# Attention with a residual and two layer norms on one Trainium2 core: the order of scores and value products, of three VectorE steps, and the engine that cuts a lower part

## The reference

```
q = x @ wq.T + bq;  k = x @ wk.T + bk;  v = x @ wv.T + bv
scores = q·k / sqrt(32), causal;  weights = softmax(scores)
x1 = layernorm(x + (weights @ v) @ wo.T + bo)
out = layernorm(x1 + quantised_scale_and_clip(x1) @ quantised_scale_and_clip(w_ffn) * rescale)
```

## Time and profile before

| | |
|---|---|
| median of 3 runs | 2452.48 us (2452.33 to 2453.8) |
| the profiled execution | 2451.5 us, of it 2449.8 us from the first to the last instruction (the span) |
| busy over the span | PE 96%, PEld 61%, DVE 76%, ACT 54%, POOL 37% |
| batches 0 to 19, without fillers | first exp at 445.41 us, first exp of batch 20 at 556.26 us |
| batches 20 to 271 | 556.26 us to about 2031 us |

### The profile page before, as it was taken

One profiled execution on the slowest core, in us unless ns is written; L12 is line 12 of the kernel. 1 busy time (PEld: TensorE's weight loads), 2 busy tenths in 40 slices (PEclk: granted clock), 3 DMA queues, 4 the chain that ended last, 5 costly groups with the idle time before them and its releaser, 6 DMA issues.

```text
span 2449.8 us, 35663 instructions
## 1 busy us (share of the span) xinstructions
PE 2347.4 (96%) x13933; PEld 1488.8 (61%) x13933; DVE 1859.7 (76%) x1387; ACT 1319.6 (54%) x1443; POOL 918.0 (37%) x472
## 2 busy tenths in 40 slices
PE   6999998789999999999999999999999998999998
PEld 5778776335555555555555555555555556888887
DVE  6655665788888888888889998888888886444444
ACT  2232224577777777777777676777777773100000
POOL 2553453013233233234232323332324323666563
PEclk9999999899999999999999999999999999999999
DMA  7775767231222112212221122212221212222221
GB/s 234 260 254 204 278 241 258 60 62 36 53 57 66 44 45 66 66 45 58 53 66 44 44 55 63 58 44 61 53 63 44 66 61 112 91 89 86 86 94 61
DMA packets 159958, 231.55 MB, mean 95 GB/s; under 512 B 9582, under 2 KB 109902, under 8 KB 157774
## 3 DMA queue, kind: packets, MB, share of 16 engines
q1 hardware_dynamic: 136206, 178.27, 25.1%
q10 hardware_dynamic: 23616, 51.39, 5.5%
HBM read 140.50 MB, written 89.13 MB: 94 GB/s over the span
## 4 chain that ended last, share of the span: by engine, by line
PE 64%; DVE 7%; ACT 5%; POOL 3%; issue 2%; DMA 0%; ACTq 0%; DVEq 0%; POOLq 0%
PE bank L1365 18%; PE bank L1377 16%; PE bank L1440 14%; PE bank L1350 12%; ACT prob L838 4%; DVE acc L1117 4%; POOL att_lo L689 2%; PE bank L1387 2%; PE bank L1430 1%; DVE acc L1113 1%; PE bank L1395 1%; POOL prob L684 1%; DVE r_den L1077 1%; ACT att_hi L825 1%; DVE r_hi L1079 0%
## 5 line engine op out<-in xcount | busy, mean ns | idle before, releaser
L838 ACT ACTIVATE prob<-bank 128x1024 f32<-128x1024 f32 x1088 | 1055.4, 1023 | 422.5 <-PE bank L1365 394.7
L1117 DVE TENSOR_TENSOR acc<-acc,prob 128x2048 f32<-128x2048 f32 x420 | 987.4, 2351 | 71.4 <-ACT prob L838 48.6
L1365 PE MATMUL bank<-q_st,keys 98*128 98x512 f32 x2176 | 646.8, 416 | 16.5 <-ACT prob L838 13.3
L1365 PEld LDWEIGHTS bank<-q_st,keys 98*128 98x128 f32 x2176 | 376.5, 189 | 352.9 <-ACT prob L838 258.4
L1377 PE MATMUL bank<-prob,v_t 128*32 128x512 f32 x4352 | 526.2, 601 | 0.0
L684 POOL TENSOR_SCALAR_AFFINE_SELECT prob<-prob 128x1024 f32<-128x1024 f32 x128 | 204.1, 1617 | 591.6 <-ACT prob L838 591.6
L1377 PEld LDWEIGHTS bank<-prob,v_t 128*32 128x32 f32 x4352 | 114.0, 109 | 263.4 <-issue 251.9
L1113 DVE TENSOR_TENSOR acc<-prob 128x2048 f32<-128x2048 f32 x60 | 141.5, 2358 | 118.5 <-ACT prob L838 78.7
L1259 PE MATMUL bank<-xt_hi,w_hi 128*128 128x512 f32 x512 | 204.8, 400 | 19.1 <-DVE xt_lo L921 15.3
L1350 PE MATMUL bank<-wo_hi,att_hi 128*128 128x512 f32 x512 | 209.1, 408 | 11.9 <-POOL att_lo L689 8.5
L869 ACT ACTIVATE xs_hi<-bank 128x1024 fp32r<-128x1024 f32 x32 | 32.9, 1027 | 336.3 <-DVE y L900 261.5
(11 more groups left out here) (132 smaller groups left out, 2643.2 us busy)
## 6 DMA issues: line engine op xcount, KB each, us to landing
q_st<-q_hi_d SPq DMA_DIRECT2D x128, 256.0 KB
xt_raw<-x_t SPq DMA_DIRECT2D x16, 1024.0 KB, 6.6
q_hi_d<-part_hi ACTq DMA_DIRECT2D x64, 256.0 KB, 2.7
q_lo_d<-part_lo ACTq DMA_DIRECT2D x64, 256.0 KB, 3.2
x_row<-x SPq DMA_DIRECT2D x32, 512.0 KB, 4.6
xb_d<-x_row SPq DMA_DIRECT2D x32, 512.0 KB, 2.7
q_st<-q_lo_d SPq DMA_DIRECT2D x64, 256.0 KB
res<-xb_d SPq DMA_DIRECT2D x32, 512.0 KB, 5.7
```

What stands on the lines that cost most here:

```text
L838: nc.scalar.activation(prob[:, s % SLOTS, 2 * p:2 * p + 2], bank[:, 2 * p:2 * p + 2], ACT.Exp, scale=SCALE).then_inc(p_done, 1)
L1117: nc.vector.tensor_tensor(acc[:, n % 2], acc[:, n % 2], new, ALU.add).then_inc(acc_done, 1)
L1365: last = nc.tensor.matmul(bank[:, g].rearrange("p (a n) -> p a n", n=P), keys[:, k // QT, k % QT * P:(k % QT + 1) * P], queries[:, :, g], ...
```

## The change

Three edits, all in attention. (1) Batches 1 to 19 and 271, which have no fillers, put the value product of step 2u-2 between the two scores of the batch. (2) VectorE's `add_residual` of both halves stands right behind the addition into `acc`, ahead of `invert` and `normalise_group`; the moments stay behind them. (3) `att_lo` is made by VectorE in the same steps (behind `normalise_group`, ahead of the moments) and no longer by GpSimd. No instruction is added or dropped.

```diff
@@ gpsimd, step loop
-                if s in split_at:
-                    q = split_at[s]
-                    pool.wait_ge(att_hi_cut, q + 1)
-                    nc.gpsimd.tensor_tensor(att_lo[q % 2][:], att[:, q % TILES_KEPT], att_hi[q % 2][:].bitcast(F32), ALU.subtract).then_inc(att_cut, 1)
@@ vector
+            def lower_attended(q):
+
+                dve.wait_ge(att_hi_cut, q + 1)
+                nc.vector.tensor_tensor(att_lo[q % 2][:], att[:, q % TILES_KEPT], att_hi[q % 2][:].bitcast(F32), ALU.subtract).then_inc(att_cut, 1)
+
             for s in range(STEPS):
...
+                if s in sum0_at:
+                    add_residual(sum0_at[s], 0)
+                if s in sum1_at:
+                    add_residual(sum1_at[s], 1)
                 if s % 2 == 0 and s // 2 in group_of_den:
                     invert(group_of_den[s // 2])
                 if s % 2 == 0 and s // 2 - 1 in group_of_den:
                     normalise_group(group_of_den[s // 2 - 1])
-                if s in sum0_at:
-                    add_residual(sum0_at[s], 0)
+                if s in split_at:
+                    lower_attended(split_at[s])
                 if s in sum1_at:
                     q = sum1_at[s]
-                    add_residual(q, 1)
                     dve.wait_ge(y_read, 2 * q + 2)
                     moments_of(res[:, q % 2], stats[:, q % 2], moments[:, q % 2], ln1, q * LN)
@@ tensor
             for u in range(BATCHES):
                 scores(2 * u)
                 between(u)
+                single = u >= 1 and u not in fillers
+                if single:
+                    weigh_values(2 * u - 2)
                 scores(2 * u + 1)
+                if u >= 1 and not single:
+                    weigh_values(2 * u - 2)
                 if u >= 1:
-                    weigh_values(2 * u - 2)
                     weigh_values(2 * u - 1)
```

More of the change, by code:

```diff
@@ L1141, in _ @@
             lower_wf(0)
-            dve.wait_ge(att_hi_cut, LAST_B + 1)
-            nc.vector.tensor_tensor(att_lo[LAST_B % 2][:], att[:, LAST_B % TILES_KEPT], att_hi[LAST_B % 2][:].bitcast(F32), ALU.subtract).then_inc(att_cut, 1)
+            lower_attended(LAST_B)
             for i in range(1, 4):
```

## The result

The changed kernel takes 2436.68 us (2435.89 to 2438.43, four runs), the kernel before 2452.4 us in four (2449.0 to 2453.8): ratio 0.9936 [0.9919, 0.9953], so it is faster by 0.6%, clear of noise. The forecast was -7.2 us; this is -15.7. The profiled execution took 2435.89 us, span 2434.1, against 2449.8 before.

What follows compares the result with a forecast made beforehand. No engine was full in batches without fillers; with fillers TensorE was the limit, 98% busy. Terms -8.5 + 3 + 3 - 7 + 2 + 0.3 = -7.2 us took 2451.5 to 2444.3, median 2445.3 us; range 2434 to 2452.

Steps and rivals of the forecast that it cites:

- Edit 1: Batches 1 to 19: value products between scores make VectorE the limit, 4.79 us a batch instead of 5.36; -8.5 us.
- The term of 0.8 for the start: Start of attention at the slow clock: a product between scores lets VectorE's addition of step 4 start 0.8 us earlier.
- Edit 3 (a): Step 4 of a pair: the lower part stands in VectorE's queue, so TensorE's filler starts 0.2 us later each; +3 us.
- Edit 3 (b): Behind step 4, VectorE's delay may last until step 12's half-0 sum, which frees the projection's bank; 0.3 in ten pairs, +3.
- Edit 3 (c): Part with fillers: GpSimd no longer stretches VectorE's additions or queues masks behind `att_lo`; -5 and -2, together -7 us.
- lower bound of -15.3: Most that the end of GpSimd's hold on VectorE could gain: TensorE's waits on `att_lo` and on the inverses.
- Edit 2: Sums first free the bank earlier but make the inverse 0.65 later where both share a step, three times late; +2 us.
- Tail: Last additions: one stretched by 0.9 under `att_lo` gives way to a lower part of 1.22; +0.3 us.
- A: Rival: nearly all stretch and mask waits in the filler part reach TensorE; -8.5 and another -10, 2434 us; chance 0.16.
- B: Rival: masks and inverses interlock with the new order, so single steps gain only 2.5 us; 2450 us; chance 0.12.
- C: Rival: VectorE's queue at step 4 delays the filler by a full 1.22, half again at step 12; +14, 2466; chance 0.06.
- D: Rival: exchange between GpSimd and VectorE doesn't help, VectorE's net load of 13.1 us falls on the path; 2457; chance 0.06.

Runs made afterwards that it cites:

- product_ahead: Changed kernel with the value product of a batch without fillers put ahead of the denominators and the spreading; 2431.33 us, ratio 0.9921.
- changed_old_sums: Changed kernel with the sums put back behind invert and normalise; 2435.82 us, ratio 0.9932 to the kernel before.
- lower_only: Kernel before with only `att_lo` moved to VectorE, behind `normalise_group`; 2437.97 us, ratio 0.9937.
- hold_read: Changed kernel in which GpSimd also does its old subtraction into a spare tile that nothing reads; 2506.13 us, ratio 1.0223.
- hold_write: Changed kernel in which GpSimd also fills a spare tile by memset, writing only; 2435.66 us, ratio 0.9936.
- best_old_sums: Changed kernel with value product ahead of denominators, first tile's split at step 3, sums back in their old place; 2430.73 us, ratio 0.9914 (2426.22 with sums first).
- lower_and_sums: Changed kernel with the old order of batches, value products not between the scores; 2439.91 us, ratio 0.9939.

## Why the prediction was right in direction and half in size

**Edit 1** (predicted -8.5; measured -7.1, and -6.8 to the first filler). Size near; a step was wrong: "VectorE doesn't ... It becomes the limit", 4.79 a batch. TensorE and ScalarE went at their own rate, 4.50 against the 4.45 I worked out, since exp waits only for the addition of four steps earlier. VectorE's lag was a debt, paid at each group's end: 1.80, 1.78 and a fall of the clock. product_ahead won 2.6 of it by covering the wait. The term of 0.8 for the start was small: the slow clock itself ended 3 to 4 us earlier, and batch 1 alone is 1.9 shorter. Batch 20's first exp stood at 551.57; less the 2.4 of the untouched stretch 549.1, just outside the 546 to 549 announced.

**Edit 3 (a)** (+3; measured +0.4 at place 3). The count was right, the filler at 0.1 behind the lower part; VectorE's four operations overlap at their ends by a little, so it was 0.08 in the pair shown instead of 0.2.

**Edit 3 (b)** (+3; measured nearly 0). Four batches grew by 0.4, and in changed_old_sums three of those got it back, so in these it was not this debt but edit 2; the fourth, 162, is the only 0.4 that lower_only shows. The wait that the debt was to lengthen, a half projection for the sum of the half before, is 3.1 us in four places in both kernels.

**Edit 3 (c)** (-7; the failed step). With (b) at zero it is -11.6 in the changed kernel, -11.9 alone. The step was "in the rest, where the split falls on an addition, 2.0 of stretch goes and 1.22 comes, worth -2 together". I netted the stretch against the new operation as two durations on VectorE. But 2.0 against 1.22 is not what counts: four additions later the stretched kernel was late for the end of a group, there met GpSimd's mask too, and the denominators or the inverse were late for TensorE; the 1.22 us ended in time. Those eleven batches gave 11.0 us and not 2. The other part of the term, four pairs with the mask right behind the split at 1.2 each, -5, was too large: there are three, and they gave 1.8 together. Nor did VectorE's waits for masks go away with `att_lo`: 39.8 us in 21 places before, 33.7 in 18 in the changed kernel, 40.3 in 21 in lower_only. My lower bound of -15.3 was made of two of TensorE's waits and left out the third row of the same view, 7.8 us of denominators waiting for the last addition, which went entirely; the inverses fell by 4.5. The wait on `att_lo`, the largest that I named, gave nothing (8.5 before; 11.3 under "issue" after).

The Trainium skill's rule ("SBUF — State Buffer", "Who interferes with whom") is borne out in both halves: hold_read's GpSimd read stretched additions to 4305 ns; beside hold_write's memset the longest is 2992, as in the changed kernel without it. The "might not help" of the Trainium skill's "Perfetto Trace Analysis", "Optimizing Scalar/DVE Operations", is not: the exchange from GpSimd to VectorE, lower_only, gave -12.0 us in batches 20 to 270.

**Edit 2** (+2; measured +0.5 inside the change, +2.5 alone by twelve runs, where falls of the clock enlarge it). The inverse was late where the prediction said, in three batches of 0.4. It missed that the earlier sum is probably worth 0.6 at place 3 once the lower part is early too (best_old_sums).

**Tail** (+0.3; measured -0.2). Within what that stretch varies.

**The rivals.** A came nearest, in size (-7.1 and -10.8 for its -8.5 and -10) and in its sign, over 6 us gained from batch 20 on. Of its mechanism the half on the stretched additions is what happened; the half on the mask waits is not, as they hardly changed. B fell (7.1 us gained before batch 20), C fell (place 3 cost 0.03 a pair, not 0.9), D fell with lower_only.

What stays open: what decides whether a wait of TensorE is followed by a fall of the clock. The spreading's 1.80 at 498.34 was not, 1.78 at 534.61 was. Nor does it take a wait of that length: the fall at 471 us in the kernel before comes among plain batches, whose longest wait is the 0.73 of the earlier trace rows.

## What to carry to other kernels

Ask of a stretched operation not how much longer it is but which semaphore the bound engine waits for next behind it: a short operation that comes out even can end in time where a stretch of like size ends late. Move an operation with two inputs off GpSimd when VectorE is about to run adds and casts whose end is waited for, or at least away from a group's end, and look again for what then comes to wait. On an engine that works in order, put independent work ahead of the instruction that waits.

## What the runs showed of the hardware

- A short wait of TensorE can cost more than itself. After waits of 1.78, 2.20 and 2.50 us the granted clock was 0.50 for 3.4 to 6.7 us, in kernels whose TensorE is about 96% busy. Falls after long waits came in some kernels and not in others at the same batch (20, 109, 245). A fall cost 1.75 us in batches 0 to 19 (lower_and_sums above). The 16 falls of hold_read in batches 20 to 270, 3.4 us each where the changed kernel has none, are some 55 us at half speed, and go with the 26 us more of busy TensorE above: by estimate over a third of its 67.8 us is clock and not waiting. The Trainium skill, "TensorE: Matmul & The Clock Gate", section "What's actually happening", has the same two levels.
- GpSimd's read stretched VectorE's cast of 128x128 from 0.23 to 2.16 us, not only operations with two inputs.
